# Softmax exponentials left in PSUM, two heads' output products in one bank, three score buffers

## The reference, cut to what matters

```python
x = L0_attn_x                                   # (1, 1024, 256)
x = x + ln(attn0(ln(x)))                        # 16 heads of 128, no mask: the stage that is changed
x = x + ln(ffn_ternary(ln(x)))                  # 256 -> 1024 -> 256
x = x + ln(latent_attention(ln(x)))             # 16 heads of 16, causal
x = x + ln(ffn_lookup(ln(x)))                   # 256 -> 688 -> 256, weights = lut[idx]

def attn0(x):                                   # S=1024, H=16, D=128
    q, k, v = split((x @ w_qkv.T))
    w = softmax(einsum('bqhd,bkhd->bhqk', q, k) * D ** -0.5)
    return einsum('bhqk,bkhd->bqhd', w, v).reshape(B, S, H * D) @ w_out.T
```

## Time and profile before

| | |
|---|---|
| median of 3 runs | 950.4 us (947.92 to 952.48) |
| time of the profiled execution | 951.13 us |
| its span, first to last instruction | 949.3 us |
| busy PE, DVE, ACT, POOL | 848.0, 789.7, 628.0, 542.8 us |
| mean granted clock of TensorE | 0.978 of full speed |

### The profile page before, as it was taken

How to read it: one execution, slowest core, us unless ns; L and a number is a source line. 1 busy time by engine, 2 the same in 40 slices (tenths; PEclk the granted TensorE clock), 3 DMA queues, 4 the chain that set the end, 5 groups by cost and what they waited for, 6 DMA issues and landing times.

```text
span 949.3 us, 13151 instructions
## 1 busy us (share of the span) xinstructions
PE 848.0 (89%) x4314; PEld 582.5 (61%) x4314; DVE 789.7 (83%) x1339; ACT 628.0 (66%) x1118; POOL 542.8 (57%) x526
## 2 busy tenths in 40 slices
PE   4799999999999998888999897679878999998996
PEld 3667767777676666556656574357654555554686
DVE  3598899999999999999999999664689787876635
ACT  3478877877867766675676668554554757667543
POOL 2124577678688788698888676461332434443301
PEclk9999999999999999999999999899979999999999
DMA  3279769868768757666676558430000000000001
GB/s 108 66 135 201 132 128 205 160 131 187 147 120 166 133 109 156 125 122 124 120 135 117 111 105 156 78 103 1 1 1 0 1 1 2 1 1 2 0 1 44
DMA packets 276851, 86.29 MB, mean 91 GB/s; under 512 B 267568, under 2 KB 272432, under 8 KB 276400
## 3 DMA queue, kind: packets, MB, share of 16 engines
q1 hardware_dynamic: 275936, 83.19, 44.4%
q0 software_dynamic: 560, 2.20, 0.7%
q10 hardware_dynamic: 288, 0.07, 0.0%
HBM read 17.29 MB, written 1.05 MB: 19 GB/s over the span
## 4 chain that ended last, share of the span: by engine, by line
DVE 44%; PE 29%; issue 10%; ACT 6%; DMA 5%; POOL 5%; SPq 1%; ACTq 0%; POOLq 0%; DVEq 0%
DVE EP L1678 14%; DVE nmax L1664 8%; DVE ptm L1751 7%; PE ps L1060 4%; DMA ET<-EP 4%; PE ps L1037 3%; PE ps L1038 3%; PE ps L1039 3%; DVE ps L1837 3%; PE ps L1074 3%; PE ps L1288 3%; PE ps L1274 3%; PE ps L1253 2%; POOL wgu L1979 2%; DVE OL L1711 2%
## 5 line engine op out<-in xcount | busy, mean ns | idle before, releaser
L1678 DVE SCALAR_TENSOR_TENSOR EP<-E,EP 128x1024 f16<-128x1024 f32 x128 | 211.9, 1675 | 8.8 <-ACT EP L1438 8.7
L1429 ACT ACTIVATE E<-ps,nmax 128x1024 f32<-128x1024 f32 x128 | 142.7, 1115 | 70.3 <-DVE nmax L1664 70.0
L1664 DVE TENSOR_REDUCE nmax<-ps 128x1 f32<-128x1024 f32 x128 | 155.1, 1212 | 4.7 <-PE ps L1039 4.6
L1961 POOL TENSOR_TENSOR XN<-XN,OT 128x256 f32<-128x256 f32 x120 | 134.0, 1138 | 23.8 <-ACT OT L1463 23.8
L1438 ACT ACTIVATE EP<-E 128x1024 f16<-128x1024 f32 x128 | 135.2, 1056 | 13.8 <-DMA ET<-EP 11.4
L1979 POOL TENSOR_TENSOR wgu<-wgu,ptm 128x688 f32<-128x688 f32 x60 | 114.3, 1904 | 38.6 <-DVE ptm L1751 38.3
L1037 PE MATMUL ps<-ET,VH 128*128 128x512 f16 x256 | 99.8, 390 | 29.6 <-DVE OL L1711 20.2
L1037 PE MATMUL ps<-KH,QH 128*128 128x512 f32 x256 | 113.1, 442 | 10.3 <-ACT E L1429 10.2
L1039 PE MATMUL ps<-KH,QL 128*128 128x512 f32 x256 | 101.6, 397 | 0.0
L1038 PE MATMUL ps<-KL,QH 128*128 128x512 f32 x256 | 101.3, 396 | 0.0
L1038 PE MATMUL ps<-ET,VH 128*128 128x512 f16 x256 | 98.2, 383 | 0.0
(11 more groups left out here) (235 smaller groups left out, 2224.9 us busy)
## 6 DMA issues: line engine op xcount, KB each, us to landing
wqr<-in_wqk SPq DMA_DIRECT2D x16, 256.0 KB, 3.9
wgu<-in_tern SPq DMA_DIRECT2D x3, 1024.0 KB, 6.2
wvr<-in_wv SPq DMA_DIRECT2D x8, 256.0 KB, 4.0
wor<-in_wo SPq DMA_DIRECT2D x16, 128.0 KB, 3.2
ET<-EP SPq DMA_TRANSPOSE x128, 4.4
X<-in_x SPq DMA_DIRECT2D x2, 512.0 KB, 5.5
prw<-in_down_idx POOLq DMA_DIRECT2D x2, 256.0 KB, 5.6
tern<-in_l_wuq_rep SPq DMA_DIRECT2D x1, 512.0 KB, 4.8
```

The costliest lines, as they stand in the source:

```text
L1429: e.activation(E[:, n % NE_RING, :], SB(BANK["scores", u, j][0]), ACT.Exp, bias=nmax[:, c:c + 1], scale=1.0, accum_out=rsum[:, c:c + 1]).t ...
L1664: e.tensor_reduce(nmax[:, c:c + 1], SB(BANK["scores", u, j][0]), AX.X, ALU.max, negate=True).then_inc(maxed.sem, 1)
L1678: e.scalar_tensor_tensor(out=EP[:, n % NE_RING, 1, :], in0=E[:, n % NE_RING, :], scalar=E_UP, in1=EP[:, n % NE_RING, 0, :], op0=ALU.mult, ...
L1961: e.tensor_tensor(XN[:, t, :], XN[:, t, :], OT[:, OT_OF[h, t][0], :], ALU.add).then_inc(o_added.sem, 1)
```

## The change

In words, part by part:

- `exp` writes back into its own score buffer in PSUM. The SBUF rings `E` and `OT` are gone.
- `row_inv` is done for each tile: DVE multiplies the row sum by 2^-15 into `rsc`, then inverts it (two dependent instructions on 128x1, before one on 128x4 per unit). `cast_e` and `rest_e` read the score buffer in PSUM and scale by this inverse, so the weights are normalised there, and `out_scale` falls away.
- A score buffer is therefore free only after `rest_e`, not after `exp`. There are three of them, banks 0 to 5.
- Work banks are 6 and 7. Bank 7 is also the bank of `attend`: from A0 to F0 only bank 6 is there for other work.
- Units are taken in another order: half 0 of two heads, then half 1 of both. `OH` and `OL` hold four units. `out_proj` adds both heads' products in one bank (12 matmuls of 256 columns, one such step per unit) and DVE adds the bank into `XN` (`out_add`).
- The string `order`, the projections' places and the ends are rewritten: A0 to A6 stand in a row at the end of a unit, A7 at the start of the next, with S0 and X0 between it and O0.
- Picks: every fourth one (v % 4 == 3) is made by POOL in place of DVE. The ternary step is a compare and a compare-and-subtract, both DVE; POOL's subtraction goes. The absolute values go to `tern`, no longer to `ptm`. The loads of the ternary weights are started from POOL's queue, not SP's.

```diff
+NWO = 3
+NSB = 3
+WB = 6
+NA = 7
 def unit(u):
-    if u >= NU - 4:
-        return H0 - 2 + u % 2, u % 4 // 2
-    return u // 2, u % 2
+    return 2 * (u // 4) + u % 2, u % 4 // 2
+
+
+def unit_of(h, half):
+    return 4 * (h // 2) + 2 * half + h % 2
...
-    for which, half in ((1, 0), (0, 0), (1, 1), (0, 1)):
+    for which, half in ((1, 0), (0, 0), (1, 1)):
         todo += project("qk", 0, which, half)
...
+    order = ("i3 f0 F0 A7 M0 p0 S0 h3 l3 e0 X0 O0 x0 S1 i0 o0 h0 y0 S2 x1 X1 l0 e1 M1 p1 w0 S3 w1 y1 p2 h1 i1 "
+             "M2 e2 p4 A0 A1 l1 i2 X2 M3 y2 A2 x2 A3 A4 A5 A6 l2 w2 p3 h2 e3").split()
+    last = ("f0 o0 w3 i3 A7 O0 L0 h3 l3 L1 F0 L2 L3 A0 L4 A1 A2 A3 w5 A4 L5 L6 L7 A5 A6 w4").split()
+    end = ("F0 o0 A7 U0 f0 O0 O1 U1 o1").split()
...
-            elif what == "A" and j < 3:
+            elif what == "A" and j < NA:
                 todo.append(("attend", u, j))
...
         def take_work(step, release):
-            i = take(step, "work", 3)
+            i = 0 if attending or last_taken[0] < last_taken[1] else 1
+            count["work"] += 1
+            last_taken[i] = count["work"]
             BANK[step] = (i, free_work[i])
             free_work[i] = release
...
             elif what == "scores":
-                i = take(step, "scores", 2)
+                i = (4 * at[0] + at[1]) % NSB
                 BANK[step] = (i, free_scores[i])
-                free_scores[i] = exped[at]
+                free_scores[i] = e_lo[at]
...
-                    if k == 0 and u > 0:
-                        w.wait_ge(*o_lo[u - 1])
+                    if k == 0:
+                        w.each([OB_FREE[u]])
...
                     for i in range(2):
-                        ts = slice((2 * g + i) * P, (2 * g + i + 1) * P)
-                        mm = three(bank[:, i * 256:i * 256 + 256], OH[:, ts], OL[:, ts],
-                                   woh[:, h % 2, :], wol[:, h % 2, :], True, True)
+                        ts = slice((2 * c + i) * P, (2 * c + i + 1) * P)
+                        for h in (2 * g, 2 * g + 1):
+                            o = unit_of(h, half)
+                            w.wait_ge(*w_lo["o", h])
+                            w.wait_ge(*o_lo[o])
+                            mm = three(bank[:, i * 256:i * 256 + 256], OH[:, o % 4, ts], OL[:, o % 4, ts],
+                                       woh[:, h % NWO, :], wol[:, h % NWO, :], h % 2 == 0, h % 2 == 1)
...
-                    e.activation(E[:, n % NE_RING, :], SB(BANK["scores", u, j][0]), ACT.Exp, bias=nmax[:, c:c + 1],
-                                 scale=1.0, accum_out=rsum[:, c:c + 1]).then_inc(exped.sem, 1)
+                    bank = SB(u, j)
+                    e.activation(bank, bank, ACT.Exp, bias=nmax[:, c:c + 1], scale=1.0,
+                                 accum_out=rsum[:, c:c + 1]).then_inc(exped.sem, 1)
...
-                    e.mul(EP[:, n % NE_RING, 0, :], E[:, n % NE_RING, :], E_UP).then_inc(e_hi.sem, 1)
+                    e.mul(EP[:, n % NE_RING, 0, :], SB(u, j),
+                          rinv[:, c:c + 1]).then_inc(e_hi.sem, 1)
...
-                    e.reciprocal(rinv[:, c:c + 4], rsum[:, c:c + 4]).then_inc(inverted.sem, 1)
+                    e.tensor_scalar(rsc[:, c:c + 1], rsum[:, c:c + 1], 1.0 / E_UP, None, ALU.mult).then_inc(sum_down.sem, 1)
+                    w.wait_ge(*sum_down[u, j])
+                    e.reciprocal(rinv[:, c:c + 1], rsc[:, c:c + 1]).then_inc(inverted.sem, 1)
...
-                    e.scalar_tensor_tensor(out=EP[:, n % NE_RING, 1, :], in0=E[:, n % NE_RING, :], scalar=E_UP,
-                                           in1=EP[:, n % NE_RING, 0, :], op0=ALU.mult,
+                    e.scalar_tensor_tensor(out=EP[:, n % NE_RING, 1, :], in0=SB(u, j),
+                                           scalar=rinv[:, c:c + 1], in1=EP[:, n % NE_RING, 0, :], op0=ALU.mult,
                                            op1=ALU.subtract).then_inc(e_lo.sem, 1)
+                elif what == "out_add":
+                    g, half, c = at
+                    t = 4 * half + 2 * c
+                    src = ps[:, WB + BANK["out_proj", g, half, c][0], :].rearrange("p (i n) -> p i n", i=2)
+                    w.wait_ge(*o_projected[at])
+                    if g == 0:
+                        w.wait_ge(*x_turned[0, 1, 1])
+                        e.tensor_copy(XN[:, t:t + 2, :], src).then_inc(o_added.sem, 1)
+                    else:
+                        w.wait_ge(*o_added[g - 1, half, c])
+                        e.tensor_tensor(XN[:, t:t + 2, :], XN[:, t:t + 2, :], src, ALU.add).then_inc(o_added.sem, 1)
...
+                        if v % 4 == 3:
+                            w.wait_ge(*index_in[t % 2][t])
+                            w.wait_ge(*lut_in[0])
+                            w.each([SUMS[step]])
+                            e.tensor_scalar(ptm[:, 1, 0:n], index_tile(t), float(v), lut[:, v:v + 1], ALU.is_equal,
+                                            ALU.mult).then_inc(picked_g.sem, 1)
```

More of the change, by code:

```diff
@@ L113, in order_of_heads @@
     for m in range(3):
[L114 to L121, removed]
+        others = [("tern_load", m)] + [("abs_sum", m, c) for c in range(4)] + [("threshold", m)]
+        others += [("ternary", m, c) for c in range(4)]
+        for step, n in zip(others, (4, 1, 1, 1, 2, 2, 1, 1, 1, 2)):
+            prep += [step] + width[:n]
+            del width[:n]
     prep += width
@@ L138, in order_of_heads @@
         if j > 0:
[L139 to L151, removed]
+            todo += [("row_inv", 0, j - 1), ("cast_e", 0, j - 1), ("rest_e", 0, j - 1)]
+        for at in first[j:j + 1 + (j == 3)]:
+            todo += project(*at)
+    todo += [("split_wo", 0), ("load_wo", 1), ("square_wv", 2)]
+    loads = []
+    order = ("i3 f0 F0 A7 M0 p0 S0 h3 l3 e0 X0 O0 x0 S1 i0 o0 h0 y0 S2 x1 X1 l0 e1 M1 p1 w0 S3 w1 y1 p2 h1 i1 "
+             "M2 e2 p4 A0 A1 l1 i2 X2 M3 y2 A2 x2 A3 A4 A5 A6 l2 w2 p3 h2 e3").split()
+    last = ("f0 o0 w3 i3 A7 O0 L0 h3 l3 L1 F0 L2 L3 A0 L4 A1 A2 A3 w5 A4 L5 L6 L7 A5 A6 w4").split()
+    end = ("F0 o0 A7 U0 f0 O0 O1 U1 o1").split()
     slots = ["p0", "p1", "p2", "p3", "p4"]
@@ L178, in order_of_heads @@
                 todo.append(({"S": "scores", "M": "max", "e": "exp"}[what], u + 1, j))
[L179 to L182, removed]
-            elif what == "A" and j < 3:
+            elif what in "ihl":
+                todo.append(({"i": "row_inv", "h": "cast_e", "l": "rest_e"}[what], u if j == 3 else u + 1, j))
+            elif what == "A" and j < NA:
                 todo.append(("attend", u, j))
@@ L624, in build @@
         wo_in.mark(0)
-        OT_OF, o_n = {}, 0
         free_sum = [None, None]
@@ L732, in build @@
             elif what == "scores":
-                i = take(step, "scores", 2)
+                i = (4 * at[0] + at[1]) % NSB
                 BANK[step] = (i, free_scores[i])
-                free_scores[i] = exped[at]
+                free_scores[i] = e_lo[at]
+            elif what == "attend" and at[1] == 0:
+                OB_FREE[at[0]] = free_work[1]
+                attending = True
+            elif what == "finish_lo":
+                free_work[1] = o_lo[at]
+                attending = False
+                count["work"] += 1
+                last_taken[1] = count["work"]
             elif what == "norm_wv":
@@ L740, in build @@
             elif what == "out_proj":
-                h, half = unit(at[0])
-                take_work(step, o_scaled[h, 4 * half + 2 * at[1] + 1])
+                take_work(step, o_added[at])
             elif what == "threshold":
```

255 lines of the change are left out of this document (103 added, 152 removed).

## The result

| | before | after |
|---|---|---|
| median of 4 runs beside each other, us | 949.4 (947.9 to 952.5) | 935.4 (934.6 to 937.7) |
| profiled execution, us; its span | 951.1; 949.3 | 935.9; 934.2 |

The ratio of after to before is 0.985 (95% interval 0.982 to 0.988): 1.5% faster, 14 to 15 us. The forecast was 919.4 us, a gain of 31.7 us. The direction and the reasons for it hold; the size is less than half.

A forecast was written before the change was run, and what follows sets the result against it. PE was taken to bound early units and DVE, slowed by POOL at SBUF, late ones. From 951.1 us, late units gave -27.4, early -1.4, the start -1.4 and the end -1.5: 919.4 us, range 902 to 944.

The forecast's parts named there:

- about 100: Sign in the profile after: POOL's busy time down by about 100 us.
- the 20 to 53 given: POOL's 28 picks: 20 to 53 us of its time, against 118 us freed.
- coupled by in-order lists I take 17.0: Every unit: both engines need 16.1 to 17.0 us, so 17.0 taken; 27.4 us less late, 1.4 early.
- already runs at 17.1 with PE 98% busy: Ground given for units of 17.0 us: the first half before the change runs at 17.1, PE 98% busy.
- The ends: Before the first scores and at the end of the stage: 1.4 and 1.5 us less.
- The -1.4 ahead of the first scores: Start of the kernel: one projection less before the first scores, 6 x 0.23 us; bounds 0 and -1.4.
- the last four adds: End of the stage: POOL's four adds, at least 0.72 us each, become two of DVE, 0.68 each: -1.5 us.
- Eaten by `row_inv`: Rival: `row_inv` in DVE's queue makes DVE stand still, units 18.0 us, 947 us in all; chance 0.17.
- its half case: Half the `row_inv` loss in DVE's queue: units of 17.5 us, 933 us in all; within that rival's chance of 0.17.
- A0 before the landing: Slower rival: PE idles at A0 for tile 3's transposes in two units of three, 966 us; chance 0.12.
- PE's floor everywhere: Rival: DVE relieved enough that every unit takes PE's 16.4 us, 903 us in all; chance 0.11.
- ACT is not hidden as the forecast had it: ACT, busy 68% of the late stretch, hides its PSUM work in slack; without that cover 0.8 us a unit.

The follow-up runs named there:

- the experiment on its source: The changed kernel with `rest_e` reading its first input from a tile in SBUF instead of the score buffer in PSUM: 962.8 us, ratio 1.013.
- both cuts: The changed kernel with `row_inv` as a single reciprocal per tile and DVE's 84 picks over 1 column: 917.8 us, ratio 0.966.
- picks one column: The changed kernel with DVE's 84 picks cut to 1 column from 512 or 688, POOL's as they are: 921.6 us, ratio 0.968.
- one reciprocal: The changed kernel with `row_inv` as one instruction, the factor 2^15 moved into the constant of the values' scale: 927.8 us, ratio 0.978.
- adds kept on POOL: The changed kernel with 112 POOL additions of 256 columns on a scratch tile put in beside the output products: 939.9 us, ratio 0.988.
- old list, adds one column: The kernel before the change with POOL's 120 adds into `XN` over 1 column in place of 256: 933.0 us, ratio 0.981.
- the swap of y2: The changed kernel with DVE's rest of the third projection put before the maximum of tile 3: 935.6 us, ratio 0.984.

## Why the prediction was right in kind and wrong in size

**Single prices: right but for POOL's.** `rest_e` 1.28 us with no spread (1.27 forecast), `out_add` 0.69 (0.68), the cast 1.10 to 1.14 (1.06 to 1.12), exp into PSUM 1.09 (1.12, bounds 1.06 and 1.25). `row_inv`'s pair starts 0.19 apart. POOL's busy time fell by 129 us ("about 100"), and luck is in that: its picks took 66 us, outside the 20 to 53 given; the adds had been 134.0 us of busy time, not 118, which took their median for the mean; and the table adds shortened by 22 us (181.3 to 159.3), which the forecast did not have. DVE needs 16.1 us of an early unit and 16.9 of a late one; the forecast had 16.1 and 17.0. Its busy time over 28 units fell by 491.5 - 461.9 = 29.6 us, of which 28.1 were forecast.

Against the Trainium skill (SBUF — State Buffer, section SBUF: two separate sides): it says that a DVE operation with two SBUF inputs and a GpSimd operation that reads SBUF exclude one another for a whole instruction. The two rows of `rest_e` in the experiment on its source fit this: same minimum, and a maximum of 1.29 against 2.66 us.

**The step that failed: "coupled by in-order lists I take 17.0".** I set a unit equal to the longer of two needs, 16.4 us of PE and 17.0 of DVE, as if lists without overtaking cost nothing at that load. Measured, late half, DVE's busy time per unit against the unit:

| kernel | DVE us | unit us |
|---|---|---|
| both cuts | 14.2 | 16.61 |
| picks one column | 14.8 | 16.72 |
| one reciprocal | 16.5 | 17.12 |
| after | 16.9 | 17.41 |
| adds kept on POOL | 17.2 | 17.81 |
| all picks on DVE | 17.8 | 18.28 |
| `rest_e` from SBUF | 18.5 | 18.81 |
| old list, adds one column | 17.9 | 18.00 |
| old list, before | 18.9 | 18.96 |

With DVE near PE's 16.6 or above it a unit of the new list takes 0.3 to 0.6 us more than DVE's own need. The old list took less than 0.1 more. The same shows early: with its adds cut the old list ran at 16.84 us with DVE busy for 15.5, the new one with 14.8 to 15.7 (both cuts, picks one column, one reciprocal) at 17.1 to 17.2. So "already runs at 17.1 with PE 98% busy" was a fact about the old list, and it was carried over to a list that had not run. The new one has it at 17.37, with A0 behind a landing and VL late at single units. In all 28 x 0.39 = 11 us of the miss.

The chains that ended last differ too. Late before the change DVE has over three quarters of it and PE no line above 0.7%; after the change PE's three lines are 47% of it (shares of the late half, before and after, cut at the end by the view):

```profile
by line: DVE EP L1678 30.2%; DVE ptm L1751 18.7%; DVE nmax L1664 16.3%; issue 13.8%; POOL wgu L1979 5.3%; DVE OL L1711 3.2%; DVE QL L1646 2.8%; DVE VL L1656 2.7%; DVE KL L1646 2.4%; POOL XN L1961 2.0%; DVE wgu L1747 0.8%; DVE rinv L1673 0.7
by line: PE ps L1033 16.0%; PE ps L1034 15.4%; PE ps L1035 15.4%; DVE nmax L1644 11.5%; issue 9.5%; DVE EP L1659 8.8%; DVE ptm L1743 6.4%; DVE VL L1636 1.8%; DVE rinv L1654 1.7%; DVE vp L1682 1.5%; DVE XN L1672 1.4%; ACT EP L1435 1.4%; DVE 
```

Then both engines wait for one another in turn, DVE mostly by way of ACT (17.6 of its 24.9 us of idle time). That the idle time is of this kind, and not of one step, the swap of y2 supports. Which part of the new list makes the difference to the old one (the longer hold of a buffer, the steps of `row_inv` between exp and cast, attend in a row, V and K just in time) stays open: no run changes one of them alone in the list as a whole.

The forecast of 17.0 would have taken PE to 98.5% (16.75 us busy) and DVE to 97.4% (16.55) at once, 196 in sum. Over the 28 units the sum was 191 before and after, and 188 to 191 in all kernels here with DVE 94% busy or more. This is no law: by halves it is 192 and 189 before, 189 and 193 after, and the calm unit of the earlier trace rows has 199.6.

**The ends.** -2.9 us forecast, +2.9 measured: 6 us more of the miss. The -1.4 ahead of the first scores came true (the first maximum starts at 29.65 us, before at 31.09), so the term "the last four adds", put at -1.5, failed: all the rest outside the 28 units took 4.3 us more. I counted the last adds by their own durations, and neither the norm's steps that now stand ahead of the last `rest_e` in DVE's list nor the wait before the last A0, which grew from 5.94 to 8.69 us with slow matmuls behind it. What share of the 4.3 each has is not shown.

**The rivals.** "Eaten by `row_inv`" came nearest: its half case, units of 17.5, was priced at 933 us. Its mechanism is shown in part, 7.5 us of the time for the second instruction. It does not hold by DVE standing still, as the rival had it: only 2.4 + 3.8 us of idle time lie before the pair. "A0 before the landing" occurs, 5.3 us in 5 waits, not in two units of three; it needs 1.6 us per unit to decide, and has 0.2. PE's floor everywhere is seen in no kernel that does all the work. The score buffers, as long as there are three, hold PE up for 0.4 us, as forecast. ACT is not hidden as the forecast had it: PE never waits for it, but DVE does.

**Where 31.7 us went.** Undone one by one, the PSUM source is worth 27 us and POOL's picks 16. Against these stand a new add per unit and four pairs of `row_inv`, (18.4 + 16.2 - 4.6 + 18.5) / 28 = 1.7 us of DVE per unit. The net relief of DVE is as forecast. What did not come is its conversion into time: 29.6 us of DVE's work gave 18.0 us of units, and the ends took 2.9 of them back.

## What to carry to other kernels

When two engines both need over 95% of a repeating unit and run a fixed order, don't take the longer need as the unit, and don't carry over how close the old order came to it: here, in the late half, the old list ran less than 0.1 us above DVE's need and the new one 0.3 to 0.6, of some 17 to 19. On such an engine tiny instructions count too: 128 of 0.14 us cost 7.5 us. Before shortening a wait in a drained end, find the longest serial chain that shares the lists: it is what sets the end once the wait is shorter.
